# A decoder on one core: relu, mask, bias, block maxima and ternary sums moved between engines, steps and queue places

## The reference

```python
# layer 0, attention, 16 heads of 128
scores = einsum('bhqd,bhkd->bhqk', q, k) / sqrt(128)
values = einsum('bhqk,bhkd->bhkd', softmax(scores), v)
x = x + values @ w_o
# layer 0, cross attention with relu features over 64 context rows per batch, 16 heads of 16
k_prime = relu(einsum('bhnd,fd->bhnf', k, Wkf)) * attention_mask[:, None, :, None]
kv = einsum('bhnf,bhne->bhfe', k_prime, v)          # v = ctx @ Wv.T + bv
k_sum = sum(k_prime, axis=2)
# layer 0, feed-forward: weights through 4 bit codes
s = max(abs(block of 64))                            # block maxima
deq = round((s - mean(s)) * qf) / qf + mean(s)       # their own codes, in blocks of 32
# layer 1, feed-forward: ternary weights
scale = max(mean(abs(w)), 1e-5); q = clamp(round(w / scale), -1, 1)
```

## Time and profile before

| | us |
|---|---|
| median of 3 runs | 922.98 (921.57 to 923.1) |
| the profiled execution | 921.72 |
| its span, first to last instruction | 919.9 |
| TensorE busy | 854.1 (93%) |
| VectorE busy | 729.0 (79%) |
| ScalarE busy | 520.4 (57%) |
| GpSimd busy | 369.3 (40%) |
| mean granted TensorE clock | 0.989 |

### The profile page before, as it was taken

The page is one execution under the profiler, slowest core; times in us unless marked ns, Lnnn a source line. Parts: engine busy times, 40 slices in busy tenths (PEclk is TensorE's granted clock), DMA queues, the critical chain, the costliest instruction groups (busy, mean ns, idle before and its releaser), DMA issues. The chain is left out here.

```text
span 919.9 us, 18693 instructions
## 1 busy us (share of the span) xinstructions
PE 854.1 (93%) x6868; PEld 633.9 (69%) x6868; DVE 729.0 (79%) x1775; ACT 520.4 (57%) x1245; POOL 369.3 (40%) x354
## 2 busy tenths in 40 slices
PE   4788988999999999999999998999988889999786
PEld 3455766777777777777777776887855578787554
DVE  6748868878888788778887775897799779887895
ACT  1435576656665666556655745464464964535556
POOL 4103456545554455455555554053233032521410
PEclk9799999999999999999999999999999999999999
DMA  9122331011101110011000000000000010000001
GB/s 279 38 71 69 54 95 35 2 35 35 34 0 34 34 34 8 27 34 34 14 21 11 1 1 1 1 2 1 1 2 1 8 40 1 1 1 1 1 1 46
DMA packets 34722, 25.56 MB, mean 28 GB/s; under 512 B 9492, under 2 KB 31596, under 8 KB 34668
## 3 DMA queue, kind: packets, MB, share of 16 engines
q1 hardware_dynamic: 34380, 24.56, 10.2%
q10 hardware_dynamic: 288, 0.26, 0.1%
HBM read 22.65 MB, written 2.17 MB: 27 GB/s over the span
## 5 line engine op out<-in xcount | busy, mean ns | idle before, releaser
L483 POOL CAST exp_hi<-exp_scores 128x1024 f16<-128x1024 f32 x64 | 67.1, 1048 | 212.5 <-ACT exp_scores L596 212.5
L485 POOL TENSOR_TENSOR exp_lo<-exp_scores,exp_hi 128x1024 f16<-128x1024 f32 x64 | 140.7, 2198 | 5.1
L596 ACT ACTIVATE exp_scores<-banks,exp_bias,unscale 128x256 f32<-128x256 f32 x256 | 141.2, 560 | 2.1
L75 PE MATMUL banks<-value_out_hi,xn_t_hi 128*128 128x256 f16 x512 | 139.6, 273 | 0.2 <-DVE X L931 0.2
L77 PE MATMUL banks<-value_out_hi,xn_t_lo 128*128 128x256 f16 x512 | 139.6, 273 | 0.0
L76 PE MATMUL banks<-value_out_lo,xn_t_hi 128*128 128x256 f16 x512 | 139.6, 273 | 0.0
L1124 PE MATMUL banks<-qk 128*128 128x256 f32 x512 | 121.6, 380 | 9.0 <-ACT exp_scores L596 8.9
L1124 PEld LDWEIGHTS banks<-qk 128*128 128x128 f32 x512 | 96.6, 190 | 30.3 <-issue 9.6
L931 DVE SCALAR_TENSOR_TENSOR X<-banks,colsum,X 128x256 f32<-128x256 f32 x256 | 106.2, 477 | 11.0 <-DVE colsum L922 9.6
L575 ACT ACTIVATE qk<-banks 128x512 f32<-128x512 f32 x128 | 75.8, 601 | 57.6 <-PE banks L77 57.6
L906 DVE TENSOR_REDUCE neg_rowmax<-banks 128x4 f32<-128x1024 f32 x64 | 78.2, 1221 | 27.9 <-PE banks L1124 27.9
(11 more groups left out here) (251 smaller groups left out, 1964.7 us busy)
## 6 DMA issues: line engine op xcount, KB each, us to landing
head_weights<-in_wqkv_d SPq DMA_DIRECT2D x32, 128.0 KB, 3.8
weight_absmax_rows<-across_partitions SPq DMA_DIRECT2D x15, 256.0 KB, 4.3
X<-in_x_d SPq DMA_DIRECT2D x4, 512.0 KB, 7.7
head_weights<-in_wqkvt_d SPq DMA_DIRECT2D x16, 128.0 KB, 3.6
head_weights<-in_w_o_d SPq DMA_DIRECT2D x16, 128.0 KB, 3.6
out<-X SPq DMA_DIRECT2D x8, 256.0 KB, 2.1
ternary_then_kv_and_rows<-in_c_fc_d SPq DMA_DIRECT2D x1, 1024.0 KB, 5.1
ternary_then_kv_and_rows<-in_c_proj_d SPq DMA_DIRECT2D x1, 1024.0 KB, 7.9
```

What stands on the lines that cost most here:

```text
L75: nc.tensor.matmul(out, lhs[0], rhs[0], start=first, stop=False)
L483: nc.gpsimd.tensor_copy(probh[:, s1_.par], prob[:, s1_.par]).then_inc(exph_ready, 1)
L485: nc.gpsimd.tensor_tensor(probl[:, s1_.par], prob[:, s1_.par], probh[:, s1_.par], ALU.subtract).then_inc(expl_ready, 1)
L596: last = nc.scalar.activation(prob[:, s1_.par, t, :], sc_ps[t // ST][:, t % ST, :], ACT.Exp, bias=nbias[:, t:t + 1], scale=unscale[:, s1_. ...
```

## The change

- Key features: the relu of L756 is made by ScalarE, into the same `kp`, after the tile's high half. The mask is no longer applied to `kp` but to `vaug`, by four GpSimd products over 128 x 544 values (`kept_values`), which stand between the reciprocal roots and the first head's low halves. A new semaphore `kept` stands before each key-values product.
- The value bias additions of `context_values` run at t = 0 to 3 of the pass, two per t, after `normalise`, rather than all before it.
- The three block maxima leave the pass and stand in step 0; the reciprocal of them in step 1; `block_sums` goes from step 0 to 2, `scale_codes` from 2 to 4, the ternary sums from 3 and 4 to 1 and 2, `LIN_MAX` from 1 to 3.
- TensorE waits for the evictions of layer 1's keys in `memory_values` rather than before the pass.
- SyncE's list: the gather of the second head's maxima and both 1 MB ternary loads come before the five stores of the block maxima; the ternary sums' exchange, the third head's gather and the fourth head's load come before the exchange of the repeated scales.

```diff
@@ -249,7 +249,7 @@
     v1_full, v1_ready = sem("v1_full"), sem("v1_ready")
-    kp_full, kp_ready = sem("kp_full"), sem("kp_ready")
+    kp_full, kp_ready, kept = sem("kp_full"), sem("kp_ready"), sem("kept_values")
     kv_full, kv_ready = sem("kv_full"), sem("kv_ready")
@@ -315,8 +315,8 @@
-    SUM_ABS, TERNARY, ROUNDING = (3, 4), 6, (7, 8)
-    LIN_MAX, KV_MAX, LIN_SCALE, KV_HI = 1, 5, 9, FIRST + ROUNDS * BODY
+    SUM_ABS, TERNARY, ROUNDING = (1, 2), 6, (7, 8)
+    LIN_MAX, KV_MAX, LIN_SCALE, KV_HI = 3, 5, 9, FIRST + ROUNDS * BODY
     view = lambda a: a.rearrange("(k p) n -> p k n", p=P)
@@ -375,6 +375,10 @@
         load_prepared(2, 0)
+        absmax_to_all(1, 2)
+        sp.wait_ge(kv_ready, NP)
+        for n, (name, kt) in enumerate((("c_fc_d", KT), ("c_proj_d", F2T))):
+            sp.dma_start(tf[n].rearrange("p (k n) -> p k n", k=kt), view(g.dram[name])).then_inc(loads_t, 16)
@@ -397,28 +401,23 @@
-        sp.wait_ge(kv_ready, NP)
-        sp.dma_start(tf[0].rearrange("p (k n) -> p k n", k=KT), view(g.dram["c_fc_d"])).then_inc(loads_t, 16)
-        absmax_to_all(1, 2)
         sp.wait_ge(nsum_ready, 2)
...
         sp.dma_start(mrows[:, :, :].rearrange("p q s -> p (q s)"), gathered(3, P, 2)).then_inc(nsum_in, 16)
-        sp.dma_start(tf[1].rearrange("p (k n) -> p k n", k=F2T), view(g.dram["c_proj_d"])).then_inc(loads_t, 16)
+        sp.wait_ge(tsum_ready, 2)
+        sp.dma_start(spread(4, P, 2), tsum[:, :]).then_inc(tsum_out, 16)
+        sp.wait_ge(tsum_out, 16)
+        sp.dma_start(trows[:, :, :].rearrange("p q s -> p (q s)"), gathered(4, P, 2)).then_inc(tsum_in, 16)
+        absmax_to_all(0, 3)
+        load_prepared(3, 1)
         sp.wait_ge(nf, NF_REP)
...
             sp.dma_start(mine, flat).then_inc(rep_in, 16)
-
-        absmax_to_all(0, 3)
-        load_prepared(3, 1)
-        sp.wait_ge(tsum_ready, 2)
-        sp.dma_start(spread(4, P, 2), tsum[:, :]).then_inc(tsum_out, 16)
-        sp.wait_ge(tsum_out, 16)
-        sp.dma_start(trows[:, :, :].rearrange("p q s -> p (q s)"), gathered(4, P, 2)).then_inc(tsum_in, 16)
         sp.wait_ge(lin_max_ready, 5)
@@ -463,8 +462,21 @@
+        def kept_values(p):
+
+            if p == 0:
+                pool.wait_ge(loads, 16 * LOADS)
+            pool.wait_ge(vaug_ready, 2 + 2 * (p + 1))
+            rows = vaug[:, p].rearrange("p a h e -> p (a h e)")
+            nc.gpsimd.tensor_tensor(rows, rows, keep0[:, p:p + 1].broadcast_to([P, 2 * XH * (XD + 1)]),
+                                    ALU.mult).then_inc(kept, 1)
+
+        rstd_of(1)
+        kept_values(0)
+        rstd_of(2)
         for p in range(1, NP):
-            rstd_of(p)
+            kept_values(p)
+        rstd_of(3)
         for a in range(2):
@@ -549,6 +561,10 @@
                 key_values(t // 4 - 1)
+            if t % 2 == 0:
+                n = t // 2
+                act.wait_ge(kp_full, n + 1)
+                nc.scalar.activation(kp[:, n // KT, n % KT, :], bank[2 + n % 2], ACT.Relu).then_inc(kp_ready, 1)
             if t % 4 == 1:
@@ -679,17 +695,18 @@
-        def context_values():
-            dve.wait_ge(second_loads, 32)
-            dve.wait_ge(cleared, 1)
-            dve.wait_ge(v0_full, NP)
+        def context_values(p):
+            if p == 0:
+                dve.wait_ge(second_loads, 32)
+                dve.wait_ge(cleared, 1)
+                dve.wait_ge(v0_full, NP)
+                for a in range(2):
+                    nc.vector.memset(vaug[a * M:(a + 1) * M, :, a, :, XD:XD + 1], 1.0).then_inc(vaug_ready, 1)
             for a in range(2):
                 rows = slice(a * M, (a + 1) * M)
-                nc.vector.memset(vaug[rows, :, a, :, XD:XD + 1], 1.0).then_inc(vaug_ready, 1)
-                for p in range(NP):
-                    nc.vector.tensor_tensor(vaug[rows, p, a, :, 0:XD],
-                                            bank[4 + p // 2][rows, p % 2 * D:(p % 2 + 1) * D].rearrange("p (h e) -> p h e", e=XD),
-                                            bv0[rows, :].rearrange("p (h e) -> p h e", e=XD), ALU.add).then_inc(vaug_ready, 1)
+                nc.vector.tensor_tensor(vaug[rows, p, a, :, 0:XD],
+                                        bank[4 + p // 2][rows, p % 2 * D:(p % 2 + 1) * D].rearrange("p (h e) -> p h e", e=XD),
+                                        bv0[rows, :].rearrange("p (h e) -> p h e", e=XD), ALU.add).then_inc(vaug_ready, 1)
@@ -739,7 +756,6 @@
         scales(0, 0)
-        context_values()
         for t in range(NT):
@@ -747,21 +763,8 @@
                 normalise(t + TP + 2)
-            if t % 2 == 0:
-                if t == 0:
-                    dve.wait_ge(loads, 16 * LOADS)
-
-                n = t // 2
-                dve.wait_ge(kp_full, n + 1)
-                nc.vector.tensor_scalar(kp[:, n // KT, n % KT, :], bank[2 + n % 2], 0.0, keep0[:, n // KT:n // KT + 1],
-                                        ALU.max, ALU.mult).then_inc(kp_ready, 1)
-            if t in (4, 6, 8):
-                dve.wait_ge(loads_n, 80)
-                block_max(t // 2 - 2)
-            if t == NT - 1:
-                dve.wait_ge(cleared, 2)
-                dve.wait_ge(block_max_ready, 3)
-                nc.vector.reciprocal(divide[:, 0:BLOCKS], s1t[:, :]).then_inc(divide_ready, 1)
+            if t < NP:
+                context_values(t)
         dve.wait_ge(mhi_ready, 1)
@@ -935,8 +938,16 @@
             if i == 0:
+                dve.wait_ge(loads_n, 80)
+                for n in range(3):
+                    block_max(n)
+            if i == 1:
+                dve.wait_ge(block_max_ready, 3)
+                nc.vector.reciprocal(divide[:, 0:BLOCKS], s1t[:, :]).then_inc(divide_ready, 1)
+            if i == 2:
+                dve.wait_ge(cleared, 2)
                 block_sums()
-            if i == 2:
+            if i == 4:
                 scale_codes()
@@ -1028,6 +1039,8 @@
                 pe.wait_ge(v1_ready, q - 1)
+            else:
+                pe.wait_ge(k1_ready, q + 1)
             own = wv1[:, :, :].rearrange("p k (j a e) -> p k a j e", a=2, e=XD)
@@ -1040,6 +1053,9 @@
             pe.wait_ge(kp_ready, 2 * p + 2)
+            pe.wait_ge(kept, p + 1)
+            if p == 0:
+                pe.wait_ge(vaug_ready, 2 * (NP + 1))
             if p >= 1:
@@ -1066,13 +1082,10 @@
         pe.wait_ge(k0_ready, KT)
-        pe.wait_ge(k1_ready, KT)
         for t in range(NT):
...
             if t % 4 == 0 and t > 0:
-                if t == 4:
-                    pe.wait_ge(vaug_ready, 2 * (NP + 1))
                 key_values(t // 4 - 1)
```

## The result

| | before | after |
|---|---|---|
| median (executions) | 923.04 (8, 920.26 to 923.40) | 924.87 (8, 923.61 to 925.75) |
| profiled execution | 921.72 | 923.61 |
| its span | 919.9 | 921.8 |
| ratio after/before | | 1.0031, 95% interval 1.0021 to 1.0041 |

The change makes the kernel slower by 0.3%, where 922.0 and "within 0.2%" had been forecast. Timed again in another batch the ratio was 1.0039 (1.0026 to 1.0052).

What follows compares the result with a forecast made beforehand. TensorE, busy 93% of 919.9 us, was taken as the bound. Setup -3.0 (loss 3.0, gain 6.0) and steps +2.0 gave -1.0: 920.7 against the profiled execution, forecast as 922.0 against the median, range 919.2 to 925.2.

Steps and rivals of the forecast that it cites:

- Part 1: Setup up to the first key-values product: it starts at 35.7 instead of 32.73, a loss of 3.0 us.
- Part 2: Setup from there to the first step: a gain of 6.0 us, first step starting at 60.5.
- the second fall: TensorE's clock drop at the second key-values product: it vanishes, product 2.0 instead of 3.7, 2.7 us gained with the features.
- Part 3: Steps 0 to 5: VectorE waits at the first ternary sum for both loads; a loss of 2.0 us.
- 5.7 + 7.9 + 0.4 = 14.0: Landing of both loads after the first step's start: data begin after the gather, run 7.9 us, 0.4 to report.
- 12.7: Alternative landing of the loads in the steps, by the skill's 358 GB/s: loss about 1.0 instead of 2.0; not used.
- The sum: Whole kernel: setup -3.0 and steps +2.0 give -1.0 us.
- three signs of being wrong: First key-values product (L1046) before 34, clock 0.50 at 46, or VectorE's longest stand at L726.
- Rival D: Step 2: block sums wait for maxima whose stores stand behind the loads; slower, 925.4 us; chance 10%.
- Rival B: Steps, before the third score product: TensorE's idle lowers its clock, costing 0.9, 922.9 us; chance 18%.
- an idle that left the clock at 1.00: Evidence against a clock fall in the steps: idle at 122 us, 1.5 of 3.4, kept full clock.
- Later work follows one for one: After the first eleven steps: later work shifts by the same amount, as nothing in it waits for the outside.

Runs made afterwards that it cites:

- bias_ahead: Changed kernel with all eight value-bias additions ahead of VectorE's tile loop and GpSimd's four mask products in a row; 917.27 us, 0.9955 of the kernel before.
- loads_first: Changed kernel with both 1 MB loads issued on SyncE ahead of the second head's weight-maxima exchange (256 KB gather); ratio 1.0000 to the kernel before.
- after_3: The changed kernel, unaltered, in a third profiled execution; first row-maximum at 69.00 us, last at 553.9.
- own_sem: Changed kernel with a semaphore for each 1 MB load, so the first ternary sum waits for c_fc alone; ratio 1.0030 to the kernel before.
- sums_34: Changed kernel with the ternary sums back in steps 3 and 4 and small maxima in step 1; 927.57 us, ratio 1.0071 to the kernel before.
- before_3: The kernel before, unaltered, in a further profiled execution; tenth to twelfth row-maximum took 15.20 us.

## Why the prediction was wrong

**Part 1, the first key-values product at 35.7: right.** 35.54, 35.81 and 36.70 in the three profiles. The mask product was put at 1.1 (1.09), the normalisations beside it at 1.15 (0.95), in the order that the text gives. That 35.54 is so near is in part luck: tile 4's low half began 0.8 earlier than put (25.69), and a pair of additions took 0.87 instead of 0.72. What the prediction did not do is ask how much of this came from where the additions stand; `bias_ahead` shows 4.2 us, and the fall of the clock besides.

**Part 2, the first step at 60.5: right in the first profile (60.20),** with the second fall gone as said. Its reference was one execution, though: the kernel before takes 1.97 to 3.65 us for the first product, by its clock, and has 68.12 to 70.85 for the first row-maximum. Between means the gain is 2.0, not 3.0.

**Part 3, the steps: here it failed.** The step that failed is the size of the stand at the first ternary sum, through its term "5.7 + 7.9 + 0.4 = 14.0" for the landing of the loads. The mechanism was named in order and place: VectorE stands at the first ternary sum for both loads, reciprocals and row-maximum queued behind it, TensorE idles before the third score product. But from the first step's start the loads came at 76.6 - 60.2 = 16.4. The first data moved where they were put, near 66. From there to the last data 7.9 was put and it took about 9, to 75; from the last data to the semaphore 0.4 was put and it took about 1.6. The first of these errors is the gather. It was given 0.9, though the earlier trace rows show it in the kernel before as 119, 168 and 153 GB/s in three slices of 0.6 us, up to 1.8. In `loads_first`, with no gather ahead, the loads' data took about 7, from 63 to 70, which is what the prediction gave them (3.1 and 3.9). Beside this stands a sentence of the Trainium skill (DMA: Bandwidth & Descriptors, Specifications), whose 358 GB/s gave 12.7: the measured 16.4 lies on the other side, and the rate was not what was wrong, as the windows show 424 GB/s at its best. From there the row-maxima were forecast at 17.95, 26.4 and 50.4 after the first step's start and came at 20.5, 27.5 and 52.2. So the steps lost 3.7 in this profile and 4.3 in the mean, not 2.0.

**The sum.** -3.0 + 2.0 = -1.0 was forecast; between the means of the profiles it is -2.0 + 4.3 + 0.6 = +2.9. Of the 3.9 between them the steps are 2.3, the start, with its one execution as reference, 1.0, and the fall in step 10, which had no term, 0.6. None of the three signs of being wrong came: they tested the mechanism, and not its size.

**Rival D, at 10%, was the nearest,** with 925.4 against 924.87, but not by its own working. In two of the changed kernel's three profiles the block sums don't stand, since the first stand, longer than forecast, just covers the return of the maxima: that was put at 22.5, or 25 in D, and the read back was issued at 81.98, 21.8 after the first step's start, to be used at 23.7. In `after_3` the stores came back later and they stand 1.36, timeline of VectorE:

```profile
87.06 0.25 DVE L743 TENSOR_REDUCE nf_row_sum<-nf_s 88x3 f32<-88x96 bf16 x1 [1.36 <-DMA nf_s<-block_scales]
```

It is what waits next, as `own_sem`, `sums_34` and `loads_first` show with 4.96, 4.80 and 5.72 us.

**Rival B, the clock falls in the steps:** it did, in all three profiles, for part of 78 to 90 us. Against it the prediction had put an idle that left the clock at 1.00; the idle of step 10, behind which the clock falls in some executions and not in others, shows that one such row is weak evidence.

**"Later work follows one for one"** holds in the mean but not between single profiles, where one fall in step 10 is 1.7 us, nearly the whole range between "faster" and "slower".

## What to carry to other kernels

When an in-order engine waits for a transfer, look for the next wait behind it before pricing its removal: shortening the first of two waits in series gave nothing in `own_sem`, and moving the work that waits a step later, with the transfers untouched, gave 0.7%. Work put between the operations of a chain costs its own length for every tile, here also that of the operations that it holds up, and the idle that this leaves TensorE cost again at the lower clock; keep it in one piece in a gap, as `bias_ahead` does. Profile an unaltered kernel several times before reading 1 or 2 us from one pair of spans.

## What the runs showed of the hardware

The clock granted after one and the same idle differs between executions of one kernel: 2.24 us of waiting in step 10 was followed by a granted clock of 1.00 in three profiles of the kernel before, and by a fall, with 0.66 in the window behind it, in `before_3`.

Five small stores of 2-byte elements took 6.56 us to issue while two 1 MB loads of the same queue were moving, and 2.79 (kernel before) or 2.85 (`loads_first`) when they were not. Their way to memory stayed long in `loads_first`: SyncE waited 9.1 us behind the last issue, in 7 of which, 76 to 83, the DMA engines moved nothing. No run gives a reason.

A 1 MB load that was alone landed 5.1 us after its issue; behind a gather of 256 KB, with a second load behind it, 7.7, and that second one 11.8; with no gather ahead (`loads_first`) the two took 6.7 and 9.1.
